# Graph block on one core: row sums eight units ahead, degrees at an earlier unit, h scaled before the last evacuation, last chunk of a panel bank by bank

## What is computed

```python
h = relu(layernorm(x))
deg = clip(adj.sum(axis=1), 1.0);  dis = deg ** -0.5
diffusion = (dis[:, None] * adj * dis[None, :]) @ h - h
sim = h @ h.T / (norm[:, None] * norm[None, :])
attn = softmax(beta * sim * adj, axis=1)
out = x + diffusion + sigmoid(alpha) * (attn @ h - h)
```

## Time and profile before

| | |
|---|---|
| median of 3 runs | 1989.08 us (1988.24 to 1989.92) |
| the profiled execution's own time | 1987.21 us |
| its span, first to last instruction | 1985.4 us |
| start, to the last transposes | 0 to 143 us |
| unit loop | 143 to about 1509 us |
| turn between the stages, TensorE idle | 17.1 us |
| diffusion stage on TensorE | 1525.8 to 1975.0 us |
| after the last matmul | 10.4 us |

### The profile page before, as it was taken

The page is one execution under the profiler, slowest core; times in us unless marked ns, Lnnn a source line. Parts: engine busy times, 40 slices in busy tenths (PEclk is TensorE's granted clock), DMA queues, the critical chain, the costliest instruction groups (busy, mean ns, idle before and its releaser), DMA issues.

```text
span 1985.4 us, 44628 instructions
## 1 busy us (share of the span) xinstructions
PE 1823.4 (92%) x19602; PEld 1408.8 (71%) x19602; DVE 1238.0 (62%) x1347; ACT 1304.8 (66%) x1259; POOL 1309.4 (66%) x788
## 2 busy tenths in 40 slices
PE   0029999999999999999999999999996999999997
PEld 0026777777777777777777777777775888888887
DVE  4677778778777877887887787787775201111110
ACT  3639989898988989988998898899886000000000
POOL 2568998999999899999999999999882000000000
PEclk9989999999999999999999999999998999999999
DMA  9347887678887678887688886788316645454520
GB/s 168 65 129 98 101 108 99 92 98 104 101 108 98 97 95 106 101 107 97 97 96 107 100 106 97 97 98 106 76 51 237 237 167 188 153 191 153 188 96 12
DMA packets 179671, 229.38 MB, mean 116 GB/s; under 512 B 8340, under 2 KB 155796, under 8 KB 174228
## 3 DMA queue, kind: packets, MB, share of 16 engines
q0 software_dynamic: 135168, 67.13, 43.7%
q1 hardware_dynamic: 26644, 151.01, 20.5%
q10 hardware_dynamic: 17664, 8.39, 1.6%
HBM read 348.13 MB, written 79.69 MB: 215 GB/s over the span
## 4 chain that ended last, share of the span: by engine, by line
PE 85%; POOL 5%; DVE 4%; ACT 3%; issue 2%; DMA 1%; SPq 0%; ACTq 0%; POOLq 0%; DVEq 0%
PE cos_ps L610 30%; PE cos_ps L669 11%; PE top_ps L669 11%; PE top_ps L640 11%; PE top_ps L644 11%; PE top_ps L642 10%; POOL ustage L286 5%; ACT arena L311 1%; ACT xe L329 1%; DMA asb<-x_in 1%; DVE vc L412 1%; DVE ssq L451 1%; SPq L207 0%; ACT xe L318 0%; DVE ssq L450 0%
## 5 line engine op out<-in xcount | busy, mean ns | idle before, releaser
L286 POOL TENSOR_TENSOR ustage<-xe,ustage 128x1024 f16<-128x1024 f32 x512 | 1094.7, 2142 | 128.0 <-ACT xe L364 122.6
L526 DVE TENSOR_TENSOR xe<-cos_ps,arena 128x1024 f32<-128x1024 f32 x512 | 626.9, 1225 | 280.9 <-PE cos_ps L610 181.5
L360 ACT ACTIVATE ustage<-xe,ebias,ab 128x1024 f16<-128x1024 f32 x512 | 635.4, 1241 | 133.0 <-DVE xe L526 131.6
L640 PE MATMUL top_ps<-h,ustage 128*128 128x129 f16 x4096 | 719.3, 221 | 2.9 <-POOL ustage L286 2.9
L644 PE MATMUL top_ps<-h,ustage 128*128 128x129 f16 x4096 | 719.2, 220 | 0.0
L642 PE MATMUL top_ps<-hlo,ustage 128*128 128x128 f16 x4096 | 718.5, 219 | 0.0
L364 ACT ACTIVATE xe<-xe,ebias,ab 128x1024 f32<-128x1024 f32 x512 | 628.2, 1227 | 0.0
L640 PEld LDWEIGHTS top_ps<-h,ustage 128*128 128x128 f16 x4096 | 400.2, 98 | 65.9 <-POOL ustage L286 3.5
L642 PEld LDWEIGHTS top_ps<-hlo,ustage 128*128 128x128 f16 x4096 | 400.1, 98 | 59.1
L644 PEld LDWEIGHTS top_ps<-h,ustage 128*128 128x128 f16 x4096 | 400.2, 98 | 0.0
L501 DVE TENSOR_REDUCE top_ps<-arena 128x8 f32<-128x1024 uint16 x256 | 311.7, 1218 | 0.0
(11 more groups left out here) (90 smaller groups left out, 1144.7 us busy)
## 6 DMA issues: line engine op xcount, KB each, us to landing
arena<-adj_in_dram POOLq DMA_DIRECT2D x256, 256.0 KB, 8.8
at_scratch<-arena SPq DMA_DIRECT2D x128, 512.0 KB, 3.8
arena<-at_scratch SPq DMA_DIRECT2D x26, 2048.0 KB, 8.0
xe<-at_scratch SPq DMA_DIRECT2D x6, 2048.0 KB, 7.9
asb<-x_in SPq DMA_DIRECT2D x16, 256.0 KB, 10.5
h_scratch<-arena SPq DMA_DIRECT2D x4, 1024.0 KB, 5.6
base_scratch<-asb SPq DMA_DIRECT2D x4, 1024.0 KB, 5.0
arena<-h_scratch SPq DMA_DIRECT2D x1, 4096.0 KB, 13.5
```

What stands on the lines that cost most here:

```text
L286: nc.gpsimd.tensor_tensor(elo[:, n % ES, :], ef[:, n % XS, :], ehi[:, n % ES, :], ALU.subtract).then_inc(elo_done, 1)
L360: nc.scalar.activation(ehi[:, n % ES, :], xm[:, n % XS, :], ACT.Exp, bias=ebias[:, 0:1], scale=ab[:, 1:2]).then_inc(ehi_done, 1)
L526: nc.vector.tensor_tensor(xm[:, n % XS, :], cos_ps[:, n % 2, :], at8[:, m % W, :, n % B], ALU.mult).then_inc(x_done, 1)
L640: nc.tensor.matmul(top_ps[:, bank, col:col + P + 1], head, h1[:, s, 0:P + 1], start=(first and t % 3 == 0), stop=final, skip_group_check=True)
```

## The change

- **Row sums.** In the first 16 units VectorE sums four extra pieces (after units 2, 6, 10 and 14), and is from then on four pieces, that is eight units, ahead: the 256th piece follows unit 500 where it followed unit 508. sum_bytes follows unit 54 of a panel where it followed unit 62.
- **Degrees.** TensorE's L622 matmuls stand before the sums of unit 506, where they stood before those of unit 511. VectorE scales and clips straight from PSUM in four instructions (clip_deg, L533 of the changed kernel) where it took four copies and two more.
- **h.** It is reloaded in two halves of 2 MB, each as soon as the rows of chunk 29 and 30 are summed and turned, into the regions that these rows leave. ScalarE scales it first, evacuates the last panel's sums after that (copy_acc) and issues the base loads last. y32 has two groups, in ptmp, where it had four in ustage. The chunk slots are renamed accordingly: slot 0 is the region of chunk 31, slots 3 and 4 are free after four and after eight groups of y.
- **Last chunk of each panel.** TensorE goes through it bank by bank: all 16 column tiles for the two output tiles of a bank, then the next bank, and counts each (tiles_done). VectorE adds a bank at a time, and signals the output after two banks; the ScalarE queue stores half a panel at a time.

```diff
-        y32 = ustage[:, :].rearrange("p (g i) -> p g i", g=4)
-        h_again = arena[:, 2 * 4096:4 * 4096].rearrange("p (s d) -> p s d", d=P)
-        slots = [arena[:, 4096:8192], arena[:, 0:4096], xe[:, :], arena[:, 8192:12288], arena[:, 12288:16384]]
+        y32 = ptmp[:, :].rearrange("p (g i) -> p g i", g=2)
+        h_again = [arena[:, 4096:8192].rearrange("p (s d) -> p s d", d=P),
+                   arena[:, 12288:16384].rearrange("p (s d) -> p s d", d=P)]
+        slots = [arena[:, 8192:12288], arena[:, 0:4096], xe[:, :], arena[:, 4096:8192], arena[:, 12288:16384]]
...
             for m in range(BLOCKS):
...
+                if m // W in (CHUNKS - 3, CHUNKS - 2) and w == W - 1:
+                    half = m // W - (CHUNKS - 3)
+                    sp.wait_ge(rows_summed, 8 * (m // W + 1))
+                    h_stored(half)
+                    sp.dma_start(h_again[half].rearrange("p s d -> p (s d)"),
+                                 h_dram[:, 4096 * half:4096 * (half + 1)]).then_inc(h_back[half], 16)
             sp.wait_ge(rows_summed, 8 * CHUNKS)
-            sp.wait_ge(h_kept, 16 * CH)
-            sp.dma_start(h_again.rearrange("p s d -> p (s d)"), h_dram).then_inc(h_back, 16)
...
-                elif k == 3:
-                    sp.wait_ge(y_scaled, PANELS)
+                elif k >= 3 and k < SL:
+                    sp.wait_ge(y_scaled, 4 * (k - 2))
...
-            copy_acc(PANELS - 1)
-            act.wait_ge(deg_ready, 1)
+            act.wait_ge(deg_ready, Q)
             nc.scalar.activation(vb[:, :], va[:, :], ACT.Sqrt).then_inc(deg_root, 1)
...
+            act.wait_ge(dis_ready, 1)
+            for g in range(PANELS):
+                if g % 4 == 0:
+                    act.wait_ge(h_back[g // 4], 16)
+                if g >= 2:
+                    act.wait_ge(y_ready, g - 1)
+                for t in range(PT):
+                    s = g * PT + t
+                    last = nc.scalar.activation(y32[:, g % 2, t * P:(t + 1) * P], h_again[s // 32][:, s % 32, :], ACT.Copy,
+                                                scale=dis[:, s:s + 1])
+                last.then_inc(y_scaled, 1)
+            copy_acc(PANELS - 1)
+            act.wait_ge(y_ready, PANELS)
             load_base(0)
             load_base(1)
-            act.wait_ge(h_back, 16)
-            act.wait_ge(dis_ready, 1)
-            for g in range(PANELS):
...
             for panel in range(PANELS):
-                act.wait_ge(out_ready, panel + 1)
                 w0, b = panel_of(panel)
                 for w in range(2):
+                    act.wait_ge(out_ready, 2 * panel + w + 1)
...
-            def copy_deg():
+            def clip_deg():
                 dve.wait_ge(deg_done, 1)
                 for q in range(Q):
-                    last = nc.vector.tensor_copy(deg[C * q:C * (q + 1), :], deg_ps[C * q:C * (q + 1), q, :])
-                link(last)
+                    nc.vector.tensor_scalar(va[C * q:C * (q + 1), :], deg_ps[C * q:C * (q + 1), q, :], 1.0 / EIGHT, 1.0,
+                                            ALU.mult, ALU.max).then_inc(deg_ready, 1)
...
-                elif n % B == 3 and n + 1 < UNITS:
-                    sum_rows((n + 1) // 16, 2 * ((n + 1) % 16 // B))
-                elif n % B == 0:
-                    sum_rows(n // 16, 2 * (n % 16 // B) + 1)
-                if n % TILES == TILES - 2:
+                elif (n % B in (0, 3) or n in (2, 6, 10, 14)) and piece < 8 * CHUNKS:
+                    sum_rows(piece // 8, piece % 8)
+                    piece += 1
+                if n % TILES == TILES - 10:
                     sum_bytes(n // TILES)
...
-                dve.wait_ge(at_used, CH * (panel + 1))
-                for part in range(2):
-                    for t in range(PT):
+                for bank in range(PT // 2):
+                    two = (2 * bank, 2 * bank + 1)
+                    dve.wait_ge(tiles_done, PT // 2 * panel + bank + 1)
+                    for part in range(2):
+                        for t in two:
...
-                if n == UNITS - 1:
+                if n == UNITS - 6:
                     degrees()
...
+                if ch < CH - 1:
+                    for j in range(16):
+                        if panel == 0 and j % PT == 0:
+                            pe.wait_ge(y_ready, 2 * ch + j // PT + 1)
+                        for t in range(PT):
+                            last = one(j, t)
+                    last.then_inc(at_used, 1)
+                else:
+                    if panel == 0:
+                        pe.wait_ge(y_ready, PANELS)
+                    for bank in range(PT // 2):
+                        for j in range(16):
+                            for t in (2 * bank, 2 * bank + 1):
+                                last = one(j, t)
+                        last.then_inc(tiles_done, 1)
```

More of the change, by code:

```diff
@@ L189, in gnn_block_kernel @@
         dis_ready = sem("dis_ready")
-        h_back = sem("h_back")
+        h_back = [sem(f"h_back{g}") for g in range(2)]
+        tiles_done = sem("tiles_done")
         y_scaled = sem("y_scaled")
@@ L569, in _ @@
                 link(last)
-                dve.wait_ge(at_used, CH * (panel + 1))
-                for part in range(2):
-                    for t in range(PT):
-                        s = tile_of(t % CH, w0 + t // CH, b)
-                        last = nc.vector.scalar_tensor_tensor(out=o[:, t, :], in0=acc2[panel % 2][:, t, part * P:(part + 1) * P],
-                                                              scalar=dis[:, s:s + 1], in1=o[:, t, :],
-                                                              op0=ALU.mult, op1=ALU.add)
-                    if part == 0:
-                        link(last)
-                link(last)
-                nc.vector.memset(gate_tmp[:, 1:2], 0.0).then_inc(out_ready, 1)
+                for bank in range(PT // 2):
[3 more added lines that the diff above has]
+                        for t in two:
+                            s = tile_of(t % CH, w0 + t // CH, b)
+                            last = nc.vector.scalar_tensor_tensor(out=o[:, t, :], in0=acc2[panel % 2][:, t, part * P:(part + 1) * P],
+                                                                  scalar=dis[:, s:s + 1], in1=o[:, t, :],
+                                                                  op0=ALU.mult, op1=ALU.add)
+                        if part == 0 or bank % 2:
+                            link(last)
+                    if bank % 2:
+                        nc.vector.memset(gate_tmp[:, 1:2], 0.0).then_inc(out_ready, 1)
         @block.tensor
@@ L661, in _, with one @@
                 if panel >= 2 and ch == 0:
-                    pe.wait_ge(out_ready, panel - 1)
+                    pe.wait_ge(out_ready, 2 * (panel - 1))
                 pe.wait_ge(at_loaded[k % SL], 16 * (k // SL + 1))
-                for j in range(16):
+                def one(j, t):
                     s = 16 * ch + j
-                    if panel == 0 and s % PT == 0:
-                        pe.wait_ge(y_ready, s // PT + 1)
-                    for t in range(PT):
-                        last = nc.tensor.matmul(acc2[panel % 2][:, t, :], slot8[k % SL][:, j // B, t * P:(t + 1) * P, j % B],
-                                                y[s // 32][:, s % 32, :],
-                                                start=(s == 0 and t % 2 == 0), stop=(s == TILES - 1), skip_group_check=True)
-                last.then_inc(at_used, 1)
+                    return nc.tensor.matmul(acc2[panel % 2][:, t, :], slot8[k % SL][:, j // B, t * P:(t + 1) * P, j % B],
+                                            y[s // 32][:, s % 32, :],
+                                            start=(s == 0 and t % 2 == 0), stop=(s == TILES - 1), skip_group_check=True)
+                if ch < CH - 1:
[5 more added lines that the diff above has]
+                    last.then_inc(at_used, 1)
+                else:
+                    if panel == 0:
[5 more added lines that the diff above has]
+                        last.then_inc(tiles_done, 1)
 def kernel(x, adj, L0_gnn_t, L0_gnn_alpha, L0_gnn_beta):
```

27 lines of the change are left out of this document (12 added, 15 removed).

## The result

| | before | changed |
|---|---|---|
| median | 1989.17 us (4 runs) | 1971.63 us (4 runs, 1971.31 to 1972.26) |
| ratio to before | | 0.9912, 95% interval 0.9895 to 0.9930 |
| profiled execution, own time | 1987.21 | 1971.31 |
| its span | 1985.4 | 1969.5 |

The change is worth 17.5 us by the medians.

What follows compares the result with a forecast made beforehand. TensorE was taken to bound the unit loop and diffusion stage, leaving gains at the turn and tail. 11.45 + 1.98 + 5.27 = 18.7 us, off the median 1989.08, gave 1970.4 us, range 1967.5 to 1974.5.

Steps and rivals of the forecast that it cites:

- Turn: From unit loop to diffusion stage: scaling no longer waits behind base loads, first diffusion matmul at 1514.35, 11.45 us earlier.
- Degrees: Degree matmuls before the last two cosines push those by 1.75 us; last mask 1.54 later, TensorE's loop ends 1.3 later.
- Row sums and SyncE queue: Unit loop and store queue: extra pieces fit VectorE's idle slots, h loads between stores delay nothing; cost 0 each.
- Bank by bank: Last chunk of each panel: new matmul order costs 0, between bounds of 0 and 167 ns per matmul.
- rival on the slower side: Bank order slows TensorE in each panel's last chunk; 18.3 ns more per matmul eats the whole gain; chance 0.04.
- Tail: Behind the last matmul: four additions and four issues instead of 16 and eight; 5.27 us less.
- Clock: Panel 0 after the turn: shorter idle stretch keeps the full clock, 1.98 us saved, bounds 0 and 1.98, little confidence.
- the clock falls all the same: Rival at the turn: half clock still comes, up to 1.98 us lost again, 1970.4 to 1972.4, most likely 1972; chance 0.36.

Runs made afterwards that it cites:

- no-lead kernel: Changed kernel with the row-sum pieces, reduction and degrees put back where they were before; 1971.86 us, ratio 0.9916.
- first run of all three: Changed kernel with degrees at unit 510 and unused matmuls added between last sums and diffusion and ahead of the unit loop's first sums; 1967.55 us, ratio 0.9895.
- tail alone: Kernel before with only the bank-by-bank last chunk, additions by banks and half stores; 1983.45 us, ratio 0.9971.

## Why the prediction was right

The forecast was 1970.4 us, the range 1967.5 to 1974.5; measured 1971.63. By its steps:

**Turn.** Last mask to first diffusion matmul: 1502.61 to 1514.35, 11.74 us, forecast; 11.73 measured. With the later last mask it is 11.50 us gained, forecast 11.45. The last sums ended 1.24 us later, counted from the first mask and without the fall in the fill (forecast 1.3). Root, dis, scaling and split came in the order and at the distances of the sum. Of the 13.02 us that this stretch lost, the base loads are 7.70, the evacuation and the clip 2.88, the lead of the row sums 2.44.

**Degrees.** 1.75 us forecast in front of the last cosines; 1.72 measured in the mask that waited, and the last mask later by 1.52 (forecast 1.54), the fall in the fill taken off. So the row sums' lead, the part of the change with the most edits, is worth 0.92 us net, as the no-lead kernel shows.

**Row sums and SyncE queue, at 0.** The masks of the no-lead kernel and of before take 1354.01 and 1354.02 us; with the degrees at unit 510 and no fall they take 1353.81 us (first run of all three, 146.59 to 1500.40). So neither the extra pieces nor the queue's order cost the loop time.

**Bank by bank, at 0.** 55.89 us a panel before and after (panels 1 to 6; the last 55.91 in both). The rival on the slower side is out.

**Tail.** 5.27 forecast, 5.43 measured in the changed kernel (10.44 us behind the last panel before, 5.01 after), 5.2 with the tail alone.

**Clock, the term that failed.** The prediction took 1.98 us saved, with little confidence, on the ground that the idle stretch would be only 0.6 us longer than the 3.7 us after which the clock had fallen before, and that so late a fall would not have its full effect. In the profiled pair 0.15 us was saved. The stretch was 4.31 us, as forecast (4.35), and in the first trace the clock did not fall inside it but 0.7 us after it, so that all of its low time fell on matmuls; in one other it fell inside, and panel 0 was slower still (58.63). The bounds 0 and 1.98 held for the changed kernel and the choice between them was wrong; the slower panel just named, behind the same 4.31 us and 0.76 us over that of before, lies outside them. The rival "the clock falls all the same", 0.36, should have been the main case. That a fall may come after the restart was not seen at all. The Trainium skill (TensorE: Matmul & The Clock Gate, why this matters for your kernels) had idle gaps of this order down as costing the clock, and the traces agree: nine of nine.

Against the profiled pair the sum closes: turn 11.50, tail 5.43, panel 0 0.15, start 0.45 earlier (first mask 146.60 against 147.05), minus 1.64 for the fall in the fill, is the 15.9 us between the spans. The medians differ by 17.5, where turn, tail and panel 0 make 17.1; the 0.4 that is left is less than medians of four executions can tell, and how often the fall in the fill comes in either kernel was not counted.

So the range holds because 16.7 of the 18.7 us (turn and tail) came as forecast, for the reasons given. That the figure is only 1.2 us off, though a term of 1.98 gave 0.15, is in part luck: the tail, 0.16 more than forecast, and this remainder went the other way.

## What to carry to other kernels

At a turn between two stages, list what stands in each engine's own order between the last input and the first use: four transfers issued ahead of a computation on the same engine cost 7.7 us, though the sums that they are added to were not done before panel 0's first bank (1562.85 in the changed kernel). Small work costs its full length in a stretch where the engine that bounds never waits (1.72 us here); put it where that engine waits anyway. A stop of TensorE of 4.3 us cost its own length and 1.7 to 2.6 us of half clock besides (panel 0 at 57.72 to 58.63 us against 56.05), and matmuls that compute nothing can be cheaper than the stop.

## What the runs showed of the hardware that was not expected

- A DMA issue on ScalarE's queue took 10.2 us at its longest in before (median 0.65), while the DMA engines were full with the SyncE queue's 10 MB (share 1.01 to 1.03 in the earlier trace rows). With the base loads behind the scaling and nothing else changed, they were issued from 1529.88 on with the DMA engines idle until then (share 0.00 from 1528 to 1530), and no issue of the sixteen took over 0.65 us. The changed kernel issues the same four transfers behind the scaling in 9.39 us, where the engines were busy again with the SyncE queue's loads (0.94 to 1.02 from 1532 to 1544); there it costs nothing, as VectorE has the base by 1545.59, ahead of the end of panel 0's first bank. The long issues go with full DMA engines in these three traces; no experiment took the SyncE queue's loads away.
- The clock fell at 1516.22 and 1517.50 us in the two traces of the changed kernel, when TensorE had been back at work for 0.7 and 0.6 us after 4.31 us idle. A clock that reads 1.00 through a gap can still fall because of it: with the gap filled it did not (1.00 from 1513 to 1519, above).
- Fall or no fall in the fill of the loop is a matter of the single execution, and moves its time by 1.64 us. The clock's rise before the loop moves it too: from the start of the last transposes to the first mask it was 7.8 us in five of the thirteen traces and 6.3 to 6.5 in the others. Single profiles of this kernel can't be compared to better than some 3 us without reading the clock at both places.
